# 86 unused TensorE products in front of a fused kernel's attention stage

## The reference, cut to what matters

```python
x = x + L0_ffn(L0_cond(x, cond_8, ...), ...)
x = x + L1_ffn(L1_cond(x, cond_8, ...), ...)

def L0_ffn(x, ...):
    h = x + gqa(rmsnorm(x, attn_norm_w), wq, wk, wv, wo)   # 16 heads of 16, 4 key/value heads, causal
    return h + moe(rmsnorm(h, ffn_norm_w), gate_w, expert_w)  # best 2 of 8 experts
```

## Time and profile before

| what | value |
|---|---|
| median of 3 runs | 2117.91 us (2117.37 to 2120.45) |
| the profiled execution | 2111.37 us |
| its span, first to last instruction | 2109.7 us |
| outside the span | 1.7 us |
| TensorE (PE) busy | 2036.1 us, 97% of the span |
| VectorE / ScalarE / GpSimd busy | 64% / 53% / 46% |
| mean granted TensorE clock | 0.976 |

### The profile page before, as it was taken

How to read it: one execution, slowest core, us unless ns; L and a number is a source line. 1 busy time by engine, 2 the same in 40 slices (tenths; PEclk the granted TensorE clock), 3 DMA queues, 4 the chain that set the end, 5 groups by cost and what they waited for, 6 DMA issues and landing times. The chain is left out here.

```text
span 2109.7 us, 50236 instructions
## 1 busy us (share of the span) xinstructions
PE 2036.1 (97%) x17544; PEld 1752.2 (83%) x17544; DVE 1347.3 (64%) x2818; ACT 1117.4 (53%) x2219; POOL 963.0 (46%) x1062
## 2 busy tenths in 40 slices
PE   7999989999999999989979999999899999999997
PEld 7999985666666666659979999999888888888886
DVE  7888954676777767765636776788654444444452
ACT  6777744666666666655543333344354444454542
POOL 0000002365565556556644444444245656565653
PEclk9999987999999999989989999999999999999998
DMA  8767711133233232229864444544344444545442
GB/s 294 264 260 267 261 59 31 62 104 96 92 108 110 87 106 96 78 92 305 300 218 144 148 151 142 175 150 151 104 96 109 95 111 95 112 96 111 96 83 30
DMA packets 134682, 289.62 MB, mean 137 GB/s; under 512 B 23026, under 2 KB 64755, under 8 KB 128243
## 3 DMA queue, kind: packets, MB, share of 16 engines
q1 hardware_dynamic: 84466, 177.25, 24.9%
q0 software_dynamic: 50048, 110.14, 20.3%
HBM read 187.17 MB, written 95.42 MB: 134 GB/s over the span
## 5 line engine op out<-in xcount | busy, mean ns | idle before, releaser
L1248 DVE TENSOR_REDUCE neg_max<-ring 128x2 f32<-128x512 f32 (+1 forms) x384 | 250.0, 681 | 106.4 <-PE ring L1734 106.1
L1041 POOL TENSOR_SCALAR_AFFINE_SELECT weights_diag<-weights_diag 128x512 f32<-128x512 f32 x256 | 158.3, 643 | 258.4 <-ACT weights_diag L1139 258.1
L2908 POOL DMA_INDIRECT out<-q_t,row_put x128 | 201.8, 1576 | 162.4 <-ACT q_t L2972 137.7
L3046 DVE TENSOR_TENSOR ex_hid<-ex_up_ps,gelu 128x512 f32<-128x512 f32 x128 | 86.9, 688 | 171.8 <-ACT gelu L2956 171.8
L2956 ACT ACTIVATE gelu<-ex_gate_ps 128x512 f32<-128x512 f32 x128 | 76.3, 596 | 187.3 <-PE ex_up_ps L62 187.3
L2379 POOL DMA_INDIRECT picked_rows<-results,lo_row_now x128 | 134.0, 1047 | 56.3 <-issue 29.8
L1139 ACT ACTIVATE weights_diag<-ring 128x512 f32<-128x512 f32 x256 | 138.5, 599 | 24.2 <-PE ring L1752 24.2
L60 PE MATMUL ex_down_ps<-ex_dn_lo,ex_hid_hi 128*128 128x256 f32 x512 | 145.1, 283 | 2.8 <-issue 2.8
L61 PE MATMUL ex_down_ps<-ex_dn_hi,ex_hid_lo 128*128 128x256 f32 x512 | 145.2, 284 | 0.0
L62 PE MATMUL ex_down_ps<-ex_dn_hi,ex_hid_hi 128*128 128x256 f32 x512 | 144.9, 283 | 0.0
L1049 POOL DMA_INDIRECT sorted_rows<-h_sb,row_now x128 | 126.8, 990 | 34.8 <-issue 31.3
(11 more groups left out here) (404 smaller groups left out, 7521.8 us busy)
## 6 DMA issues: line engine op xcount, KB each, us to landing
ug_raw<-in_w_ug SPq DMA_DIRECT2D x32, 1028.0 KB, 5.0
dn_raw<-in_w_dn SPq DMA_DIRECT2D x32, 640.0 KB, 5.2
q_t<-sorted_rows SPq DMA_DIRECT2D x136, 128.0 KB
moe_w<-in_expert_gu SPq DMA_DIRECT2D x16, 1024.0 KB, 4.8
results<-c0n POOLq DMA_DIRECT2D x33, 256.0 KB, 4.4
x_raw<-in_x_t SPq DMA_DIRECT2D x32, 256.0 KB, 5.1
c0n<-c SPq DMA_DIRECT2D x32, 256.0 KB, 4.3
c0r<-c SPq DMA_DIRECT2D x32, 256.0 KB
```

What stands on the lines that cost most here:

```text
L1041: nc.gpsimd.affine_select(part, part, [[0, G], [1, P]], ALU.is_ge, 0.0, base=0, channel_multiplier=-1).then_inc(kept_done, 1)
L1248: nc.vector.tensor_reduce(out, src, AX_X, ALU.max, negate=True).then_inc(max_done, 1)
L2908: nc.gpsimd.indirect_dma_start(out=out_rows, out_offset=bass.IndirectOffsetOnAxis(ap=at, axis=0), in_=eo[c][:, n, :], in_offset=None, comp ...
L3046: nc.vector.tensor_tensor(hid[f % 2][:], up_ps[f % 2][:], gelu[f % 2][:], ALU.mult).then_inc(hid_done, 1)
```

## The change

A function `extra_products` is added to TensorE's program of the attention stage. It is called once, behind the waits for constants and in front of body -1. It issues 86 products into the ring banks 0 to 3 and waits for the last of them on a new semaphore. Nothing reads their results, and the scores overwrite the banks.

```diff
@@ -1775,6 +1776,36 @@
+            def extra_products():
+                plain = at.wqk_raw[:].rearrange("p k c s -> p (k c s)")
+                rounded = at.wqk_hi[:].rearrange("p k c s -> p (k c s)")
+
+                def tiles(weights, rows, columns, high=32):
+                    for g in range(P // high):
+                        own = slice(high * g, high * g + rows)
+                        nc.tensor.matmul(ring[g][:, 0:columns], weights[own, 0:P], weights[own, P:P + columns], start=True, stop=True)
+
+                for n in range(3):
+                    tiles(plain, HD, 512)
+                for n in range(3):
+                    tiles(plain, HD + 1, 512)
+                for n in range(3):
+                    tiles(plain, HD + 1, 256)
+                for n in range(3):
+                    tiles(rounded, 32, 512)
+                for n in range(3):
+                    tiles(rounded, 32, 256)
+                for n in range(3):
+                    tiles(rounded, 32, 128)
+                for n in range(3):
+                    tiles(rounded, 48, 512, 64)
+                for n in range(4):
+                    nc.tensor.matmul(ring[0][:], rounded[:, 0:P], rounded[:, P:P + 512], start=(n == 0), stop=(n == 3))
+                for n in range(4):
+                    last = nc.tensor.matmul(ring[n % 2][:], rounded[:, 0:P], rounded[:, P:P + 512], start=True, stop=True)
+                last.then_inc(extra_done, 1)
+                pe.wait_ge(extra_done, 1)
@@ -1899,6 +1930,7 @@
             pe.wait_ge(at.w_lo_done, at.LOWS)
+            extra_products()
             over_batches(body)
```

More of the change, by code:

```diff
@@ L819, in attention_phase @@
         scores_done = sem("scores_done")
+        extra_done = sem("extra_done")
         max_done = sem("max_done")
```

## The result

The changed kernel takes 2132.36 us, the median of 6 runs (2122.66 to 2137.64), beside 2117.64 us for the kernel before in 6 runs of the same sessions (2115.41 to 2120.45). The medians differ by 14.7 us. The ratio estimated from the single runs is 1.0062, 95% interval 1.0038 to 1.0085: slower, by 8 to 18 us. The forecast was 2134.8 us, in a range of 2125 to 2143.

A forecast was written before the change was run, and what follows sets the result against it. TensorE, busy 97% of the span, was taken as the bound. Added products cost 20.4 us cold, -1.5 and -0.3 for the clock, +0.4 wait: 19.0; less 2.1 returned, +16.9 on 2117.91 gives 2134.8 us, range 2125 to 2143.

The forecast's parts named there:

- The verdict: Whole kernel: slower by over 0.2%, given 91%; within 0.2% had 6%, faster 3%.
- the cold for a property of the place: Behind the barrier, before the first scores: added work begins 0.3 us before the clock falls to 0.50, doubling its price.
- Plain tiles, 13.1 us: Start of the addition: 36 plain products in 9 rounds, all at clock 0.50, 1.71 us per round of 512 columns.
- the 0.3 us for the ends of a group: Within the plain tiles' 13.1 us: 0.3 us paid once, beside 12.8 us for the rounds.
- Rounded tiles of 32 rows, 2.6 us side by side: In the addition: 36 rounded products in 9 rounds, four tiles running together at 0.50; one by one 10.2 us.
- The clock inside the addition: Clock falls after 0.3 us (-0.3), stays 0.50 over plain tiles, rises within rounded ones, last 3.0 cold us halved (-1.5).
- their 3.9: Rounded row tiles in the addition, side by side at 0.50: 2.6 us for 32 rows and 1.3 for 48 rows.
- What comes back, 2.1 us: At the first maxima of body -1: TensorE's wait shrinks, by 2.6 us at clock 1.00 or 1.5 at 0.50.
- Sum, 16.9 us: Whole kernel: 19.0 us of addition less 2.1 us that come back, added to the median.
- Case B: In the addition: solid work of any form raises the clock within 4.6 us; +10.6, 2128.5 us; chance 18%.
- Case C: In the addition: rounded row tiles do not run side by side; +8.9, about 2144 us; chance 10%.
- Case D: Bodies -1 and 0: added work keeps the clock at 1.00, giving back 16.5 us; 2114.6 us in all; chance 7%.

The follow-up runs named there:

- rounded only: Changed kernel with only the 42 rounded products on row tiles kept, and the wait: 2115.0 us, ratio 1.0 to the kernel before.
- whole array only: Changed kernel with only the 8 rounded products over the whole array kept, and the wait: 2113.72 us, ratio 1.0 to the kernel before.
- plain last: Changed kernel with the same 86 products reordered: whole array first, then rounded row tiles, then plain tiles: 2123.31 us, ratio 1.0042 to the kernel before.
- the addition twice: Changed kernel with all the added products issued two times in a row: 2138.9 us, ratio 1.0105 to the kernel before.
- filled further: Kernel before, no addition, with 51 unused whole-array products in TensorE's waits ahead of the barrier and in bodies -1 and 0: 2101.09 us, ratio 0.994.
- the changed one with its waits filled: Changed kernel plus unused whole-array products in TensorE's waits, 6 + 5 ahead of the barrier and 12 in body -1: 2117.63 us, ratio 1.0015.
- before, waits filled: Kernel before, no addition, with 27 unused whole-array products in TensorE's waits, 6 + 5 ahead of the barrier, 16 in body -1: 2111.46 us, ratio 0.9985.

## Why the prediction was right

The verdict holds, and so do the main steps: the plain tiles ran cold, the rounded ones side by side, and a part came back at the second scores. One premise was right for this order only. The prediction took the cold for a property of the place, where the kernel before had it; with rounded products first the clock stayed at 1.00 there (rounded only, whole array only, plain last). The forecast came out because the added products begin with the plain tiles. Term by term:

*Plain tiles, 13.1 us.* Measured 310.37 - 298.67 = 11.7 to the first rounded start, which falls among the last plain ones; counted to the end of the last plain group, 12.1. With 0.9 us at full speed in it that is 12.6 to 12.9 in cold terms. Their starts lie 1.71 us per round of 512 columns, as derived (two groups of records, each 0.853 us behind the last). Of the 0.3 us for the ends of a group about 0.1 was there.

*Rounded tiles of 32 rows, 2.6 us side by side.* Yes. At 0.50 rounds of 512 columns lie 0.43 us apart in the changed kernel, as forecast. At 1.00 one takes 0.234 us, where one by one it would be 0.85, a gain of 3.65. The Trainium skill's 3.07 ("TensorE: Matmul & The Clock Gate", "Measured speedup vs the span model") would have been 0.28 us. Case C, tiles one by one, is refuted.

*The clock inside the addition.* It fell 0.9 us behind the start instead of 0.3 and rose at 313.2, among the rounded products, as was said. The last 3.2 us ran warm; without the wait that is about 2.8 us of work, which gives back 2.8 us and not 1.5. These two and the plain tiles make the addition shorter, 17.7 us instead of 19.0, though the rounded row tiles took some 0.6 us more, in cold terms, than their 3.9. How soon the clock falls is not fixed by the program: in the four profiles in which plain tiles stand behind the unfilled barrier it fell 0.9, 1.5, 2.3 and 2.6 us behind their start. That this term missed by 0.6 us and not by 2.3 is luck.

*What comes back, 2.1 us.* Measured 17.8 - 15.0 = 2.8, a little above the 2.6 for a warm start. The runs with rounded products alone add what the prediction did not say: the first 2.1 to 2.6 us of added work here were free.

*Sum, 16.9 us.* Measured 15.0 and 15.1 us at the second scores, 14.7 and 15.8 in the medians. The sum was 1 to 2 us too high, by the terms above. The first profiled execution was 2133.37 us, not the 2128.3 that the sum gives for one like that of before, because of the longer cold stretch and the creep.

*Case B, solid work of any form brings the clock back soon.* Refuted: 8.1 us of solid plain tiles did not, nor 10.8 us in the changed kernel. Behind rounded products that followed them it rose, 2.8 and 4.2 us after their start in the two profiles of the changed kernel and 2.1 us in the addition twice. The advice of the Trainium skill to keep TensorE busy ("TensorE: Matmul & The Clock Gate", "Why this matters for your kernels") agrees with these traces for holding the clock, and for raising it with rounded products, not for raising it with plain row tiles of 16 and 17 rows. Whether it is the 16 and 17 rows or the plain form that counts was not tried: no run has plain products that fill the array, or rounded ones on 16 rows.

*Case D, the warm start.* It did not come about by the addition, for the reason given: the clock was lost in the wait for the maxima (320.0). Its price of 16.5 us was not reached either: in the kernel before, filled further, bodies -1 and 0 warm save 12.1 us. Body 0 took 16.7 us rather than 15 and body -1 16.2 rather than 13.3; the fillings in them are a part of that.

What the prediction did not have is how far single executions differ. Of 12 runs of the changed kernel three stand apart, at 2117.32, 2122.66 and 2124.62 us, the rest between 2126.99 and 2137.64. The three have a mean clock of 0.979, 0.977 and 0.976, the others 0.970 to 0.973; a mean higher by 0.004 is about 17 us less at the low level. Of the kernels whose clock was held at the barrier, the changed one with its waits filled keeps close together (2116.13 to 2118.97 in ten runs), the others do not (before, waits filled: 2107.53 to 2114.52 in eleven; filled further: 2097.87 to 2105.72 in six). That in the three fast runs the clock did not fall ahead of or in the plain tiles is possible, but none of them was profiled, and it stays open.

## What to carry to other kernels

Before pricing work on TensorE, read the granted clock at the place where it will stand, and what TensorE did just before: the same 86 products cost 17.7 or 11.2 us by their order, and 11.1 us in the old order once two gaps of 1.6 and 1.8 us ahead of them were filled. Where TensorE must wait, unused products over the whole array can be worth more than they cost (51 of them gained 13.8 us here), up to the point where they delay the next step (67 gained 9.0). And look for the first wait behind an addition; it returns what fits into it. Only what does not fit is paid, so the costs of parts tried one by one need not add up.

## What the runs showed of the hardware that was not expected

Holding the clock and raising it are different things. Plain row tiles of 16 and 17 rows, back to back, kept a level of 1.00 for 6.4 us (second copy of the addition) and left a level of 0.50 where it was for 8.1 and 10.8 us. A gap of 1.7 us at the barrier was followed by a fall where plain tiles stood behind it, in four profiles of four, and by none before the next wait where rounded products did, in three of three. Rounded products on 32-row tiles run four at a time, 0.234 us per round of 512 columns at 1.00. And the falls of the clock in bodies -1 and 0 cost the kernel before 12 us: 11 short products ahead of the barrier kept the first one off, 40 more in the waits behind it the others.
